# Tables for the first dequantised weights of a transformer block: zeros unpacked once, scale parts in four pieces, fewer warming transposes

## The reference

```
W[k, n] = scales[g_idx[k], n] * (w4[k, n] - (z4[g_idx[k], n] + 1))   # gate, up: 4 groups, 1376 columns
h = silu(xf @ Wg) * (xf @ Wu)
out = h @ Wd                                                         # down: 10 groups, 512 columns
```

## Time and profile before

| what | value |
|---|---|
| runs, median | 862.51 us (861.14 to 863.62) |
| the profiled execution's own time | 862.04 us |
| its span | 860.2 us |
| PE busy | 833.5 us, 97% |
| VectorE busy | 486.7 us, 57% |
| GpSimd busy | 248.7 us, 29% |

### The profile page before, as it was taken

One profiled execution on the slowest core, in us unless ns is written; L12 is line 12 of the kernel. 1 busy time (PEld: TensorE's weight loads), 2 busy tenths in 40 slices (PEclk: granted clock), 3 DMA queues, 4 the chain that ended last, 5 costly groups with the idle time before them and its releaser, 6 DMA issues.

```text
span 860.2 us, 10709 instructions
## 1 busy us (share of the span) xinstructions
PE 833.5 (97%) x4012; PEld 677.5 (79%) x4012; DVE 486.7 (57%) x824; ACT 272.4 (32%) x469; POOL 248.7 (29%) x202
## 2 busy tenths in 40 slices
PE   4789999999999999999999999999999999999998
PEld 3567777887888888788888888888887888888786
DVE  5777765465745453464876787545445744434452
ACT  3123342354512111232565684112112511112121
POOL 5533441474201514130325444141510201101100
PEclk9799999999999999999999999999999999999999
DMA  6557656886484444241314336854445154444121
GB/s 166 178 174 250 205 196 217 288 318 239 171 326 144 154 148 145 77 144 52 111 50 149 96 113 251 325 168 138 155 121 168 46 201 154 145 161 143 44 98 50
DMA packets 71152, 139.37 MB, mean 162 GB/s; under 512 B 24428, under 2 KB 35332, under 8 KB 66108
## 3 DMA queue, kind: packets, MB, share of 16 engines
q1 hardware_dynamic: 65884, 131.32, 45.6%
q10 hardware_dynamic: 5088, 6.95, 2.4%
q0 software_dynamic: 128, 0.41, 0.2%
HBM read 100.63 MB, written 37.95 MB: 161 GB/s over the span
## 4 chain that ended last, share of the span: by engine, by line
PE 72%; DVE 2%; ACT 1%; issue 0%; POOL 0%; DVEq 0%; ACTq 0%; POOLq 0%
PE ps L762 36%; PE ps L769 33%; PE ps L780 2%; PE ps L1165 1%; DVE xn L1687 1%; DVE pT L1653 0%; ACT pr L1513 0%; POOL t L2156 0%; ACT oT L1280 0%; DVE oT L1653 0%; DVE t L1653 0%; DVE hT L1653 0%; PE ps L1091 0%; DVE mx L1993 0%; ACT xn L1285 0%
## 5 line engine op out<-in xcount | busy, mean ns | idle before, releaser
L762 PE MATMUL ps<-blk,ring 128*128 128x512 f32 (+1 forms) x1386 | 320.9, 389 | 0.1
L762 PEld LDWEIGHTS ps<-blk,ring 128*128 128x128 f32 (+1 forms) x1386 | 256.7, 185 | 58.1 <-DVE blk L1653 0.5
L769 PE MATMUL ps<-wd,hT 128*128 128x512 f32 (+1 forms) x1056 | 250.8, 392 | 0.8 <-DVE hT L1653 0.7
L769 PEld LDWEIGHTS ps<-wd,hT 128*128 128x128 f32 (+1 forms) x1056 | 196.8, 188 | 43.5 <-DVE hT L1653 1.1
L2199 POOL TENSOR_TENSOR h<-h,u 128x512 f32<-128x512 f32 (+1 forms) x33 | 42.7, 1293 | 325.9 <-ACT h L1406 325.9
L769 PE MATMUL ps<-xT,wp 128*128 128x512 f32 x480 | 120.8, 409 | 0.3 <-DVE xT L1653 0.3
L769 PEld LDWEIGHTS ps<-xT,wp 128*128 128x128 f32 x480 | 92.4, 196 | 22.9 <-issue 2.7
L1656 DVE TENSOR_TENSOR u<-ps,p1s 128x512 f32<-128x512 f32 (+1 forms) x66 | 45.4, 688 | 97.3 <-PE ps L762 97.2
L1406 ACT ACTIVATE h<-h 128x512 f32<-128x512 f32 (+1 forms) x33 | 20.9, 632 | 176.8 <-DVE h L1656 176.8
L1656 DVE TENSOR_TENSOR u<-ps,u 128x512 f32<-128x512 f32 (+1 forms) x66 | 45.6, 691 | 25.6 <-PE ps L762 24.6
L1656 DVE TENSOR_TENSOR h<-ps,p1s 128x512 f32<-128x512 f32 (+1 forms) x33 | 22.8, 691 | 64.1 <-PE ps L762 64.1
(11 more groups left out here) (128 smaller groups left out, 897.5 us busy)
## 6 DMA issues: line engine op xcount, KB each, us to landing
ring<-wsaved SPq DMA_DIRECT2D x29, 1024.0 KB, 5.2
ring<-wsaved SPq DMA_DIRECT2D x33, 768.0 KB, 4.4
wsaved<-wp SPq DMA_DIRECT2D x10, 1024.0 KB, 4.9
stream<-xres SPq DMA_DIRECT2D x32, 256.0 KB, 2.7
xn<-stream SPq DMA_DIRECT2D x8, 1024.0 KB, 8.0
xres<-stream SPq DMA_DIRECT2D x32, 256.0 KB, 3.6
wfull<-wf ACTq DMA_DIRECT2D x20, 256.0 KB, 2.4
wsaved<-wp SPq DMA_DIRECT2D x10, 512.0 KB, 3.0
```

The lines of the kernel that those rows point to most:

```text
L762: mm = pe.matmul(ps[0:w, bank, :], ring[:, slot, which, a, kt, 0:w], blk[:, which, b, kt, :], start=not onto and kt == 0 and n == 0, stop= ...
L769: mm = pe.matmul(bank_ap, lhs(a), rhs(b), start=first and n == 0, stop=last and n == 2)
```

## The change

The zeros of gate and up are loaded flat (32 rows of 43 words), unpacked once in nine steps at the head of VectorE's queue, and sent by two DMAs from there to their table rows. Those of down are unpacked just before them and loaded by ScalarE's queue. Indices are copied to 36 rows a matrix, and `clamp`, `compare_low` and `one_hot` of gate and up take rows 0 to 99 only, all three on VectorE. GpSimd makes piece 0 of the scales in four steps around its two powers. The others are pieces of 2, 3 and 4 tiles, made in rounds 0, 2 and 4 by two steps each. PE does 6 warming transposes in place of 12 at its head, one more between those of x and two behind `scales_zeros(1)`; `scales_zeros(2)` moves into the first product. Two of the four low parts of x come before unit 1. (`spread` and `rows_hi` change in their arguments only.)

```diff
--- before.py
+++ after.py
@@ -175,13 +175,18 @@
-        TAB_TILES = ((0, 2), (2, 5), (5, NT))
-        TAB_COLS = (NT - 5) * P
-        S_ROWS, Z_ROWS = slice(0, FOLD + 3 * GK), slice(0, FOLD + Z_ROW + GK)
+        TAB_TILES = ((0, 2), (2, 4), (4, 7), (7, NT))
+        TAB_COLS = (NT - 7) * P
+        HOT_ROWS = Z_ROW + GK
+        S_ROWS, H_ROWS = slice(0, FOLD + 3 * GK), slice(0, FOLD + HOT_ROWS)
         sc_gu = scratch("sc_gu", [P, INTER], F32)
         left_gu = scratch("left_gu", [P, TAB_COLS], F32)
-        zq_gu = scratch("zq_gu", [P, INTER // PACK], I32)
-        zi_gu = scratch("zi_gu", [P, TAB_COLS // PACK, PACK], I32)
+        ZP = 16
+        ZC = GK * INTER // PACK // ZP
+        zq_gu = scratch("zq_gu", [P, ZC], I32)[0:2 * ZP, :]
+        zi_gu = scratch("zi_gu", [P, ZC, PACK], I32)[0:2 * ZP, :, :]
+        zs_gu = scratch("zs_gu", [P, ZC * PACK], BF16)[0:2 * ZP, :]
         keep = scratch("keep", [P, 2], F32)
...
@@ -440,12 +446,11 @@
...
             return step
-        CUT_STEPS, ZERO_STEPS, SCALE_STEPS = 5, PACK + 1, 2
-        ZEROS_D_DONE = 2 * ZERO_STEPS + SCALE_STEPS
-        TAB_DONE = (ZERO_STEPS + SCALE_STEPS, ZEROS_D_DONE + ZERO_STEPS + SCALE_STEPS,
-                    ZEROS_D_DONE + 2 * (ZERO_STEPS + SCALE_STEPS))
+        FIRST_STEPS, CUT_STEPS, ZERO_STEPS, SCALE_STEPS = 4, 5, PACK + 1, 2
+        def tab_done(piece):
+            return 2 * ZERO_STEPS + SCALE_STEPS * piece
         def cut_scales(eng, step, sc, rest, rest2, parts):
@@ -461,29 +466,37 @@
...
             step(lambda: eng.tensor_scalar(zb, zi.rearrange("p c j -> p (c j)"), 1.0, None, ALU.add))
-        def zeros_gu(eng, step, piece):
+        def scale_cols(piece):
             first, end = TAB_TILES[piece][0] * P, min(TAB_TILES[piece][1] * P, INTER)
-            words = (end - first) // PACK
-            unpack_zeros(eng, step, zq_gu[Z_ROWS, first // PACK:end // PACK], zi_gu[Z_ROWS, 0:words, :], zb_gu[Z_ROWS, first:end])
+            return sc_gu[S_ROWS, first:end], left_gu[S_ROWS, 0:end - first], tab_gu[S_ROWS, first:end]
+        def first_left_gu(pool, step):
+            s, left, _ = scale_cols(0)
+            step(lambda: pool.tensor_scalar(left, upper(s), keep[S_ROWS, 0:1], None, ALU.mult))
+            step(lambda: pool.tensor_tensor(out=left, in0=left, in1=s, op=ALU.subtract))
+        def first_table_gu(pool, step):
+            _, left, dst = scale_cols(0)
+            step(lambda: pool.tensor_scalar(dst, upper(left), keep[S_ROWS, 1:2], None, ALU.mult))
+            step(lambda: pool.tensor_tensor(out=dst, in0=dst, in1=left, op=ALU.subtract))
         def scales_gu(eng, step, piece):
-            first, end = TAB_TILES[piece][0] * P, min(TAB_TILES[piece][1] * P, INTER)
-            s, left, dst = sc_gu[S_ROWS, first:end], left_gu[S_ROWS, 0:end - first], tab_gu[S_ROWS, first:end]
+            s, left, dst = scale_cols(piece)
             step(lambda: eng.scalar_tensor_tensor(out=left, in0=upper(s), scalar=keep[S_ROWS, 0:1], in1=s,
...
                                                   op0=ALU.mult, op1=ALU.subtract))
...
@@ -599,26 +612,25 @@
             for m in range(2):
-                sp.dma_start(idx[FOLD * m:FOLD * m + FOLD, GU_COLS], spread(g_idx[m])).then_inc(d_idx_gu, 16)
-            sp.dma_start(grp[:, :], groups).then_inc(d_grp, 16)
+                sp.dma_start(zq_gu[m * ZP:(m + 1) * ZP, :], flat(zeros[m], ZC)).then_inc(d_zq_gu, 16)
             sp.wait_ge(s_cst, 1)
             for m in range(2):
-                row = FOLD * m + Z_ROW
-                sp.dma_start(zq_gu[row:row + GK, :], zeros[m]).then_inc(d_zq_gu, 16)
+                sp.dma_start(idx[FOLD * m:FOLD * m + HOT_ROWS, GU_COLS], spread(g_idx[m], HOT_ROWS)).then_inc(d_idx_gu, 16)
+            sp.dma_start(grp[:, :], groups).then_inc(d_grp, 16)
             sp.wait_ge(s_cst, 2)
...
             sp.dma_start(shift[:, :], shifts).then_inc(d_small, 16)
-            load_units(sp, [1])
-            sp.dma_start(zq_d, flat(zeros[2], ZC_D)).then_inc(d_zq_d, 16)
-            load_units(sp, [2, 3])
-            sp.wait_ge(s_cut, CUT_STEPS)
-            table_d(sp, 0, range(3))
+            sp.wait_ge(s_tab, 2 * ZERO_STEPS)
+            for m in range(2):
+                row = FOLD * m + Z_ROW
+                sp.dma_start(zb_gu[row:row + GK, :], zs_gu[m * ZP:(m + 1) * ZP, :]).then_inc(d_zb, 16)
+            load_units(sp, [1, 2, 3])
+            sp.wait_ge(s_cut, FIRST_STEPS + CUT_STEPS)
+            table_d(sp, 0)
             load_units(sp, [4, 5])
-            sp.wait_ge(s_tab, ZEROS_D_DONE)
-            table_d(sp, 0, (3,))
             for u in range(UNITS):
@@ -833,13 +845,16 @@
...
                 if m == 2 and i < 2:
-                    pe.wait_ge(s_oh, 3 + i)
+                    pe.wait_ge(s_oh, 4 + i)
                 if m == 2 and i in (0, D_TILES):
                     pe.wait_ge(d_tab[1 if i else 0], 64)
-                if m == 0:
+                if u == 0:
+                    pe.wait_ge(d_zb, 32)
+                    pe.wait_ge(s_cut, FIRST_STEPS)
+                if m == 0 and i:
                     for piece, (first, _) in enumerate(TAB_TILES):
                         if i == first:
-                            pe.wait_ge(s_tab, TAB_DONE[piece])
+                            pe.wait_ge(s_tab, tab_done(piece))
                 if u:
...
@@ -865,7 +880,9 @@
...
                     if i == 0:
-                        plain_product(0, 0, 0, by_tile=True)
+                        plain_product(0, 0, 0, (0, 1), True)
+                        scales_zeros(2)
+                        plain_product(0, 0, 0, (2, 3), True)
                         pe.wait_ge(s_wlo, made(1, 0))
...
@@ -1055,18 +1072,20 @@
...
             pe.wait_ge(d_small, 32)
-            keep_warm(12)
-            pe.wait_ge(s_oh, 2)
+            keep_warm(6)
+            pe.wait_ge(s_oh, 3)
             scales_zeros(0)
             for r in range(RT):
+                if r == 2:
+                    keep_warm(1)
                 pe.wait_ge(s_ln[0], r + 1)
...
             scales_zeros(1)
-            scales_zeros(2)
+            keep_warm(2)
             plain_top()
...
@@ -1472,6 +1491,7 @@
...
                     copy(x_turned(a)[:, 0, k, :], ps[:, TURN_BANK[k], :]).then_inc(s_ahi, 1)
+            act.dma_start(zq_d, flat(zeros[2], ZC_D)).then_inc(d_zq_d, 16)
             for r in range(RT):
...
@@ -1483,9 +1503,8 @@
...
             w_hi(0)
-            rows_hi(0, (0, 1, 2))
+            rows_hi(0)
             w_hi(1)
-            rows_hi(0, (3,))
             plain_top()
...
@@ -1722,9 +1741,9 @@
                 minus(blk[:, what, 1, kt, :], blk_f[:, what, 1, kt, :], f32(blk[:, what, 0, kt, :])).then_inc(s_slo34, 1)
-            def rows_lo(t):
+            def rows_lo(t, kts=range(KT)):
                 dst = (xT0, xT1)[t]
-                for k in range(KT):
+                for k in kts:
                     bank = TURN_BANK[k] if t else 4 + k
...
@@ -1770,16 +1789,14 @@
...
                     if i == 0:
-                        dve.wait_ge(s_ohd, 3)
+                        dequantise(3)
+                        dve.wait_ge(s_ohd, 2)
                         one_hot(dve, hots, DOWN_FIRST, 1, oh_d[:, 0:P])
-                        unpack_zeros(dve, tables, zq_d, zi_d, zb_d.rearrange("p c j -> p (c j)"))
-                        dequantise(3)
                     if i == 1:
-                        dve.wait_ge(s_ohd, 5)
+                        dve.wait_ge(s_ohd, 4)
                         one_hot(dve, hots, DOWN_REST, 1, oh_d[:, P:D_COLS])
-                    if i == 2:
-                        zeros_gu(dve, tables, 2)
-                        scales_gu(dve, tables, 2)
+                    if i in (2, 4):
+                        scales_gu(dve, tables, 2 if i == 2 else 3)
                     dve.wait_ge(s_up, i + 1)
...
@@ -1794,11 +1811,11 @@
...
                         ln_shift(1)
+                    if i == 0:
+                        scales_gu(dve, tables, 1)
                     plain_lo(0, i)
...
                         dequantise(4)
-                        zeros_gu(dve, tables, 1)
-                        scales_gu(dve, tables, 1)
                         dequantise(5)
...
@@ -1955,29 +1972,28 @@
...
             hots = maker(dve, s_oh)
+            dve.wait_ge(d_zq_d, 16)
+            unpack_zeros(dve, tables, zq_d, zi_d, zb_d.rearrange("p c j -> p (c j)"))
+            dve.wait_ge(d_zq_gu, 32)
+            unpack_zeros(dve, tables, zq_gu, zi_gu, zs_gu)
             dve.wait_ge(d_idx_gu, 32)
-            clamp(dve, hots, GU_COLS, GK)
-            ln_stats(0, (0,))
-            dve.wait_ge(d_zq_gu, 32)
-            zeros_gu(dve, tables, 0)
-            ln_stats(0, (1,))
+            clamp(dve, hots, GU_COLS, GK, H_ROWS)
+            ln_stats(0, (0, 1))
             ln_var(0, (0, 1))
...
             ln_var(0, (2, 3))
-            dve.wait_ge(d_cut_gu, 32)
-            dve.wait_ge(s_cst, 5)
-            scales_gu(dve, tables, 0)
```

(44 more changed lines are left out.)

## The result

The changed kernel took 854.43 us (median of 4 runs, 853.72 to 856.05) against 863.07 (4 runs, 861.14 to 863.86): ratio 0.9906, 95% interval 0.9883 to 0.9929, so 8.6 us faster. The profiled execution is the slowest of the four: 856.05 us with a span of 854.2, 6.0 less than the span before. So the trace accounts for 6.0 us, not for 8.6; the kernel before was profiled 1.0 us under its median, the changed one 1.6 over its own. The four executions fall into two pairs: 853.72 and 853.88 us, with a mean granted clock of 1.0 (the higher level throughout, as far as the profile's row shows it), and 854.98 and 856.05, with 0.996 and 0.997.

A forecast was written before the change was run, and what follows sets the result against it. PE, busy 833.5 of 860.2 us, was taken as the bound. Gains of 3.9 (stall with opening), 2.1 (its tail) and 3.9 (round 2), 9.9 us, took 862.04 to 852.1; with 0.47 for the median, 852.5, range 849 to 857.

The forecast's parts named there:

- signs that I had named: No PE wait over 1.5 us between 20 and 80, first product at 19.0, 12 matmuls in about 3.1, among others.
- rival B: Round 0: weight tile 4 comes late, PE waits 3 us, the clock falls again, the opening yields nothing: 857; chance 0.19.
- The opening: Up to the first product: it starts at 19.0, 1.6 us before 20.57.
- The stall: Round 0, PE waiting for VectorE: ends at 32.9 against 36.76, 3.9 us with the opening's gain in it.
- The tail: Behind the first stall: the clock stays up and 12 matmuls take 3.06 for 5.19, 2.1 us.
- Round 2: Third scale piece split over two rounds, so PE's second wait and its tail go: 3.9 us.
- Round 4: Round with two scale steps on 480 columns and two LayerNorm statistics: without room, a cost of up to 1 us.
- The low clock at the first product: PE waits some 1.5 us in three gaps there, so the low clock was expected again.
- rival A: Opening: PE's gaps are short enough, the clock stays up and the stall ends at 31.3: 851.0; chance 0.20.
- The Trainium skill's rule (GPSIMD Engine Reference, Key points): GpSimd shares SBUF interfaces with VectorE and collides with it; would slow the opening's statistics by at most 0.9 us.
- Rival D: With half the warming transposes, PE stays at the lower clock past the opening: slower, 865.5; chance 0.03.
- The rule of the Trainium skill named there (TensorE: Matmul & The Clock Gate, Part 1): PE's lower clock is the default, released by activity; by it alone the first 6 matmuls are slow, 1.1 us more.

The follow-up runs named there:

- `one_piece`: Changed kernel with the last two pieces of the scales made as one of 7 tiles in round 2: 854.28 us.
- `warm12`: Changed kernel with 12 warming transposes at the head in place of 6: 855.82 us.
- `pool_waits`: Changed kernel with one wait added: GpSimd starts weight tile 3's low part only after VectorE's low part of the first hidden tile: 852.64 us.
- `tile4_first`: Changed kernel with the low part of the first hidden tile behind weight tile 4 on VectorE, not ahead of it: 851.71 us.
- `dve_scales`: Changed kernel with the first piece of the scale table made by VectorE in two steps, not by GpSimd in four: 853.31 us.
- `best`: Changed kernel with the first hidden tile's low part behind weight tile 4 and the first scales on VectorE: 851.52 us.
- `opening_old`: Changed kernel with 12 warming transposes, first scales on VectorE and x's four low parts behind weight tile 1, as before: 856.14 us.
- `dve_x_after`: Changed kernel with first scales on VectorE and the old order of x, all four low parts behind weight tile 1: 854.23 us.

## Why the prediction was right, and where it was not

The time and the range held: 854.4 for 852.5. The gain was 8.6 for a forecast of 10.0. What made the gain is what was forecast: the two waits for VectorE went from 4.6 and 2.3 us to 2.2 and 0.6. The first zeros step came early, and `tab_gu` is no longer waited for in the loop. But most of the signs that I had named did not come. There is a wait of PE of 2.2 us where none over 1.5 should be, the first product at 20.77 and not 19.0, 12 matmuls in 4.37 and not 3.1, the clock low from 34 to 37 us, and late waits of 0.6 and 0.5 us at 52.7 and 76.5. The profiled execution is nearest to rival B, 857, with both causes that it names, the late first table and GpSimd's collision: the opening yields nothing, and the clock falls again. The median comes as near to the forecast as 1.9 us since two of the four executions were faster, with a mean granted clock of 1.0, by all signs those in which the clock stayed up behind the stall. I forecast that for a wait of 1 us; with one of 2.2 it is luck. The sum itself ends at 852.6, not 852.5 (862.04 - 9.9 + 0.47). By its steps, in the profiled execution:

- *The opening, 1.6 us forecast, -0.2 measured.* The step that failed is GpSimd's. I had the scales land at 9.5 and four steps of 0.9, and named the lateness, 14.2 to 15.1; it was 15.7, with table steps of 1.20 and 1.04. And I took 18.9 for the first product from weight tile 0's low part, while the transposes of x ran at the lower clock to 19.7, VectorE's first low part of x waited behind them until 19.74, and that low part of weight tile 0 itself ended at 20.10. The zeros were no burden: their loads, first in the queues, landed within 1.8 us, before 3.0, where I had taken 6.
- *The stall, to end at 32.9; 34.0 measured.* I had put GpSimd's collision on the two scale steps (1.0 to 1.9 us). They took 0.95 together, though GpSimd's one-input index step ran beside them (28.30 to 30.71); it fell on the next step instead, the low part, which I had at 0.7 and which took 1.74. The size I had allowed for was right, its place was not, and the place shows the cure.
- *The tail, 2.1; 0.8 measured,* since PE waited 2.2 and not 1 us. The same wait in `one_piece` left the clock up, and in `warm12` the 12 matmuls took 5.49: this term differs between executions by up to 2.5 us. The granted clocks of the four runs (1.0 in 853.72 and 853.88, less in the others) suggest that it is most of their spread of 2.3 us; only one of them has a trace.
- *Round 2, 3.9; 3.3 measured.* PE still waited 0.58, behind 1.53 us for the second scale step and 0.75 for the save: a DMA wait that I had not in the sum. *Round 4, up to 1 allowed as a risk; 0.75 lost.*
- *The low clock at the first product*, which I took as likeliest, did not come: the six matmuls at 20.77 took 1.64. That half of rival A came true, and the time that it should bring was lost to the late start.
- The Trainium skill's rule (GPSIMD Engine Reference, Key points) was set at a cost of at most 0.9 us in the opening. It decided in round 0 instead, at 1.05 us for one step, and came again at 49.12, 68.85 and 82.70. `pool_waits` bears it out for a step with both operands in the data memory. Steps with one operand in PSUM go by unhindered: at 27.40 `wf` took 0.69 in the changed kernel beside a low part from 26.92.
- Rival D did not come. The rule of the Trainium skill named there (TensorE: Matmul & The Clock Gate, Part 1) made its point, where it did, on the transposes of x: with twelve warming ones eight took 1.09 and 1.04 us, with six 1.97 and 1.92. But the same opening gave 1.09 and 1.36 in `tile4_first`, so six are sometimes enough. By 20.77 the clock was up with either.

## What to carry to other kernels

Ask of each step on the critical queue not only how long it is but whether another engine's step will be running when it starts; moving it behind one that is not disturbed gave more here (2.7 us) than the smaller pieces did. Take a repeated preparation out of the loop before making it smaller: the split alone was worth nothing. When an opening becomes faster, look in the next rounds for what takes the gain back: here the clock behind the stall in `dve_scales`, and a wait for a save in `best`. And look at the granted clock of every run, not of the profiled one alone, before a median is explained from one trace.

## What the runs showed that I had not expected

A VectorE step that starts together with a two-input step of GpSimd's, or just behind it, is held until about that one's end, not slowed in proportion. The step from 30.88 takes 1.74 us and ends 0.5 behind GpSimd's at 32.09; the scale step of 0.61 us alone took 1.53 and ended 0.4 behind; one of 0.48 alone took 1.59 in `opening_old` and `dve_x_after`. The one-input index step of 2.4 us did much less: beside it the two scale steps took 0.47 and 0.48, one small shift 0.69 for 0.17, and the one-hot of 128 columns 0.80 where it took 0.34 in the kernel before. A load of 3 KB issued first in a queue landed in 1.6 us, the same kind of load issued at 3.03 in 5.0. And the PEclk row of the kernel before reads 1.00 up to the first fall, also from 11 to 14.7, when the records of the warming transposes took 421 ns each and not 274: in the opening the durations tell the clock, not the row.
